# Two residual attention layers: diagonal blocks of a key-value product in column tiles, their copies on ScalarE, and pieces cut in two

## The reference

```python
xn = _ln(x, ln_w, ln_b)                                    # layer 0
q = softmax((xn @ Wq + bq).reshape(b, t, h, dh), axis=-1)
k = softmax((xn @ Wk + bk + (1 - mask) * -1e6).reshape(b, t, h, dh), axis=1)
v = ((xn @ Wv + bv) * mask).reshape(b, t, h, dh)
att = einsum('bnhd,bnhl->bhdl', k, v)
y = einsum('bnhd,bhdl->bnhl', q, att).reshape(b, t, d)
scale, shift = split((silu(emb) @ W_emb + b_emb)[:, None, :], 2, axis=2)
hh = _ln(y, ln2_w, ln2_b) * (1 + scale) + shift
x = x + silu(hh) @ W_out + b_out
# layer 1: the same frame, with att = softmax(q @ k.T + mask), y = att @ v, H = 16
```

## Time and profile before

| | |
|---|---|
| median of 3 runs | 870.1 us (869.51 to 870.53) |
| profiled execution, span | 869.6 us |
| TensorE busy | 825.9 us, 95% |
| VectorE busy | 786.1 us, 90% |
| ScalarE busy | 709.8 us, 82% |
| GpSimd busy | 732.7 us, 84% |
| granted TensorE clock, mean of the span | 0.987 |

### The profile page before, as it was taken

How to read it: one execution, slowest core, us unless ns; L and a number is a source line. 1 busy time by engine, 2 the same in 40 slices (tenths; PEclk the granted TensorE clock), 3 DMA queues, 4 the chain that set the end, 5 groups by cost and what they waited for, 6 DMA issues and landing times.

```text
span 869.6 us, 25205 instructions
## 1 busy us (share of the span) xinstructions
PE 825.9 (95%) x8653; PEld 590.2 (68%) x8653; DVE 786.1 (90%) x1610; ACT 709.8 (82%) x1250; POOL 732.7 (84%) x1214
## 2 busy tenths in 40 slices
PE   9998788999999999999999999999999999999885
PEld 4487666677777777777677777777777776656443
DVE  6898899999999999999999999999998999998962
ACT  6457847897889798888888888888888788998794
POOL 6769999799999989989999999988998887887314
PEclk8899989999999999999999999999999999999998
DMA  8221464435352525343534434334453333444311
GB/s 224 77 38 40 118 109 103 105 76 116 98 134 56 143 76 105 90 121 100 125 97 82 132 86 111 91 103 114 85 130 106 78 84 85 112 123 103 103 31 37
DMA packets 149306, 85.84 MB, mean 99 GB/s; under 512 B 87478, under 2 KB 141852, under 8 KB 149180
## 3 DMA queue, kind: packets, MB, share of 16 engines
q1 hardware_dynamic: 149180, 84.23, 39.5%
HBM read 39.52 MB, written 25.79 MB: 75 GB/s over the span
## 4 chain that ended last, share of the span: by engine, by line
PE 47%; POOL 18%; DVE 15%; issue 10%; ACT 4%; DMA 3%; SPq 2%; POOLq 0%; DVEq 0%; ACTq 0%
PE banks L690 12%; PE banks L837 7%; DVE NM L1274 6%; PE banks L698 5%; PE banks L824 4%; PE banks L813 4%; PE banks L705 3%; POOL Z L1933 2%; PE banks L720 2%; POOL ZHL L1940 2%; PE banks L847 2%; DVE st L1175 2%; POOL AB L2004 2%; PE banks L756 2%; POOL ZHL L1937 2%
## 5 line engine op out<-in xcount | busy, mean ns | idle before, releaser
L1274 DVE TENSOR_REDUCE NM<-banks 128x4 f32<-128x1024 f32 x256 | 302.5, 1212 | 9.5 <-PE banks L813 8.4
L1696 ACT ACTIVATE wraw<-banks,uu 128x1024 f32<-128x1024 f32 x154 | 170.2, 1136 | 22.3 <-PE banks L824 21.4
L1696 ACT ACTIVATE PX<-banks,uu 128x1024 f32<-128x1024 f32 x102 | 113.6, 1138 | 14.5 <-PE banks L824 12.8
L690 PE MATMUL banks<-wo,SH 128*128 128x256 f16 x768 | 96.1, 277 | 7.6 <-POOL SH L1978 7.2
L1920 POOL TENSOR_TENSOR rs<-ve,nhalf 128x2 f32<-128x2 f32 x128 | 90.2, 705 | 10.6
L813 PE MATMUL banks<-SK,SQ 51*128 51x256 f16 x1024 | 88.8, 273 | 7.0 <-DVE NM L1274 3.1
L824 PE MATMUL banks<-SQ,SK 53*128 53x256 f16 x1024 | 88.4, 272 | 6.9 <-DVE NM L1274 2.0
L690 PE MATMUL banks<-wv,ZT 128*128 128x256 f16 x768 | 94.5, 273 | 0.3 <-DVE AT L1224 0.2
L1978 POOL TENSOR_TENSOR SH<-ST,SH 128x512 f16<-128x512 f32 x64 | 74.3, 1168 | 22.9 <-ACT SH L1664 22.9
L690 PEld LDWEIGHTS banks<-wo,SH 128*128 128x128 f16 x768 | 73.2, 99 | 24.4 <-POOL SH L1978 10.5
L1678 ACT ACTIVATE R<-banks,fcs,sqs 128x256 f32<-128x256 f32 x128 | 73.8, 577 | 19.4 <-PE banks L698 19.2
(11 more groups left out here) (187 smaller groups left out, 1925.2 us busy)
## 6 DMA issues: line engine op xcount, KB each, us to landing
scr<-AB SPq DMA_DIRECT2D x64, 256.0 KB, 2.5
X<-in_x_dram SPq DMA_DIRECT2D x32, 256.0 KB, 2.9
SQ<-scr SPq DMA_DIRECT2D x64, 128.0 KB, 2.7
SK<-scr SPq DMA_DIRECT2D x64, 128.0 KB, 2.8
out_dram<-wemb SPq DMA_DIRECT2D x32, 256.0 KB, 2.5
SQ<-scr SPq DMA_DIRECT2D x64, 64.0 KB, 2.8
SK<-scr SPq DMA_DIRECT2D x64, 64.0 KB, 2.8
wemb<-in_L_cond_emb_w_dram SPq DMA_DIRECT2D x1, 1024.0 KB, 5.3
```

Of the source, the lines that this page charges most:

```text
L690: m = PE.matmul(dst[:, t, :], zt[:, j, k, t * P:(t + 1) * P], w[:, i, k, :], start=(k, n) == (0, 0), stop=(k, n) == (1, 2))
L1274: V.tensor_reduce(NMe[:, c, :, 2 * g:2 * g + 2], banks[:, n:n + 2, :].rearrange("p a (h m) -> p a h m", m=T), AX.X, ALU.max, negate=True). ...
L1696: A.activation(px(v % 5), banks[:, n:n + 2, :].rearrange("p a n -> p (a n)"), ACT.Exp, scale=uu[:, 0:1]).then_inc(S["exp"])
```

## The change

- `att`: only the diagonal blocks. For each half f and each token tile c, four products of 32x32 (j = 0 to 3), each writing 32 partitions and 32 columns of the bank, 16 products in place of 4.
- `at_` moves from VectorE to ScalarE: four copies of 32 partitions put the blocks on the diagonal of AT, whose other entries are set to zero once. The mask `blk` is gone. The keys' reciprocal sums are now applied in `qt`, in two halves with a scale per partition; `qt` waits for `rk` too.
- Pieces in two: statistics `s` and their aggregation `a` (VectorE); `r` loses the negated mean and the variance to ScalarE's new `n`; `z` becomes `c`, `h`, `z` (GpSimd), with one Z buffer for each layer; `km` leaves its scaling to GpSimd's `kn`, `np_` its first half to GpSimd's `nh`; `rq` is cut into `qd` and `rq`, `Y1_` into `rd` and `Y1_`.
- Setup: `mb3` and `mh3` share memory with PX2; constants `epa` are new.
- All five lists, the setup's order and the tables BANK and FREED are written anew. Their lines are left out below.

```diff
--- before.py
+++ after.py
...
         ident = sb("ident", [P, P])
-        blk = sb("blk", [P, P])
...
+        ve = sb("ve", [P, 2, 4, 2])
+        epa = sb("epa", [P, 2])
         nm = sb("nm", [P, 2, 4, 2])
         rs = sb("rs", [P, 2, 4, 2])
-        Z = sb("Z", [P, 2, D])
+        Z = sb("Z", [P, 2, 2, D])
...
             def x_in(b):
-                e.wait_ge(S["z0"], up(b - 2))
+                e.wait_ge(S["c0"], up(b - 2))
                 e.wait_ge(S["xb0"], up(b - 2))
                 e.dma_start(X[:, b % 3, :, :], x[b].rearrange("(t p) d -> p t d", p=P)).then_inc(d_x[b % 3], 16)
...
-                        m = PE.matmul(banks[:, n, f * P:(f + 1) * P], KTs[:, o, c, f * P:(f + 1) * P],
-                                      V0s[:, o, c, f * P:(f + 1) * P], start=(c == 0), stop=(c == 1))
+                        for j in range(4):
+                            h = slice(f * P + 32 * j, f * P + 32 * j + 32)
+                            m = PE.matmul(banks[32 * j:32 * j + 32, n, 32 * f:32 * f + 32], KTs[:, o, c, h], V0s[:, o, c, h],
+                                          start=(c == 0), stop=(c == 1))
                 m.then_inc(S["att"])
...
+            pv(4, 4); att(11); pv(4, 5); rows(6, 3); cols(4, 7); y0(10); y0T(9); y1T(3); rows(6, 4); rows(6, 5)
...
             def stats(b, l, src):
-                e.wait_ge(S[f"s{l}"], b)
+                e.wait_ge(S[f"a{l}"], b)
                 for t in range(2):
                     i = V.bn_stats(st[:, l, t, :], src[:, t, :])
-                follow(i)
+                i.then_inc(S[f"s{l}"])
+
+            def moments(b, l):
+
+                e.wait_ge(S[f"s{l}"], b + 1)
+                e.wait_ge(S[f"n{l}"], up(b - 1))
                 for t in range(2):
                     i = V.bn_aggr(mv[:, b % 2, l, t, :], st[:, l, t, :])
-                i.then_inc(S[f"s{l}"])
+                i.then_inc(S[f"a{l}"])
...
             def km(b):
                 e.wait_ge(S["k0"], b + 1)
-                e.wait_ge(S["ke"], b)
-                follow(V.tensor_reduce(kmx[:, :], bank(home("gk0", b)), AX.X, ALU.max, negate=True))
-                V.tensor_scalar(kmx[:, :], kmx[:, :], un[:, 1:2], None, ALU.mult).then_inc(S["km"])
+                e.wait_ge(S["kn"], b)
+                V.tensor_reduce(kmr[:, :], bank(home("gk0", b)), AX.X, ALU.max, negate=True).then_inc(S["km"])
...
             def rk(b):
                 e.wait_ge(S["ke"], b + 1)
+                e.wait_ge(S["qt"], up(b - 1))
                 V.reciprocal(rks[:, b % 2], ks[:, :]).then_inc(S["rk"])
...
+            def qd(b):
+                e.wait_ge(S["qe"], b + 1)
+                e.wait_ge(S["rq"], b)
+                V.tensor_reduce(qsum[:, :], heads(QE), AX.X, ALU.add).then_inc(S["qd"])
+
             def rq(b):
-                e.wait_ge(S["qe"], b + 1)
-                follow(V.tensor_reduce(qsum[:, :], heads(QE), AX.X, ALU.add))
+                e.wait_ge(S["qd"], b + 1)
+                e.wait_ge(S["Y0"], up(b - 1))
                 V.reciprocal(rqs[:, b % 2], qsum[:, :]).then_inc(S["rq"])
...
-            def at_(b):
-                e.wait_ge(S["att"], b + 1)
-                e.wait_ge(S["rk"], b + 1)
-                e.wait_ge(S["y0"], b)
-                for f in range(2):
-                    i = V.scalar_tensor_tensor(out=AT[:, f, :], in0=banks[:, home("gat", b), f * P:(f + 1) * P],
-                                               scalar=rks[:, b % 2, f:f + 1], in1=blk[:, :], op0=ALU.mult, op1=ALU.mult)
-                i.then_inc(S["at"])
-
...
             def np_(b):
-                e.wait_ge(S["max"], 8 * b + 8)
-                if b == 0:
-                    ready(e, "nmz")
-                else:
-                    e.wait_ge(d_nt[(b - 1) % 2], 16 * ((b - 1) // 2 + 1))
-                follow(V.tensor_scalar(NMp[:, :, 0, :], NM[:, :, :], 2.0 ** -15, None, ALU.mult))
+                e.wait_ge(S["nh"], b + 1)
                 V.scalar_tensor_tensor(out=NMp[:, :, 1, :], in0=NM[:, :, :], scalar=2.0 ** -15, in1=NMp[:, :, 0, :],
                                        op0=ALU.mult, op1=ALU.subtract).then_inc(S["np"])
 
+            def rd_(b, h):
+                v = banks[:, home(f"gty{h}", b), :].rearrange("p (c h f) -> p c h f", c=2, f=32)
+                e.wait_ge(S["ty"], 2 * b + h + 1)
+                if b >= 1:
+                    e.wait_ge(S["Y1"], 2 * b + h - 1)
+                V.reciprocal(rd[:, h], v[:, :, :, 16]).then_inc(S["rd"])
+
             def Y1_(b, h):
-                n = home(f"gty{h}", b)
-                e.wait_ge(S["ty"], 2 * b + h + 1)
+                e.wait_ge(S["rd"], 2 * b + h + 1)
                 e.wait_ge(S["yn1"], b)
-                v = banks[:, n, :].rearrange("p (c h f) -> p c h f", c=2, f=32)
-                follow(V.reciprocal(rd[:, h], v[:, :, :, 16]))
+                v = banks[:, home(f"gty{h}", b), :].rearrange("p (c h f) -> p c h f", c=2, f=32)
                 V.tensor_tensor(Y[:, 1].rearrange("p c (u h f) -> p u c h f", u=2, f=16)[:, h], v[:, :, :, 0:16],
                                 rd[:, h].unsqueeze(3).to_broadcast([P, 2, 8, 16]), ALU.mult).then_inc(S["Y1"])
...
+            def mean_of(b, l):
+                k, a = l % 2, (ZS ** -2, 1.0)[l % 2]
+                e.wait_ge(S[f"a{l}"], b + 1)
+                e.wait_ge(S[("c0", "yn0", "c1", "yn1")[l]], up(b - 1))
+                first(e, b, "cst")
+                A.activation(nm[:, b % 2, l, :], mv[:, b % 2, l, :, 0], ACT.Copy, scale=-1.0)
+                A.activation(ve[:, b % 2, l, :], mv[:, b % 2, l, :, 1], ACT.Identity, bias=epa[:, k:k + 1],
+                             scale=a).then_inc(S[f"n{l}"])
...
             def ke(b):
-                e.wait_ge(S["km"], b + 1)
+                e.wait_ge(S["kn"], b + 1)
...
             def qt(b):
                 e.wait_ge(S["qtT"], b + 1)
                 e.wait_ge(S["y0"], up(b - 1))
-                A.activation(QTs[:, b % 2], bank(home("gqt", b)), ACT.Identity).then_inc(S["qt"])
+                e.wait_ge(S["rk"], b + 1)
+                for f in range(2):
+                    i = A.activation(QTs[:, b % 2, f], bank(home("gqt", b))[:, f, :], ACT.Copy, scale=rks[:, b % 2, f:f + 1])
+                i.then_inc(S["qt"])
+
+            def at_(b):
+                first(e, b, "cst")
+                e.wait_ge(S["att"], b + 1)
+                e.wait_ge(S["y0"], b)
+                for j in range(4):
+                    h = slice(32 * j, 32 * j + 32)
+                    i = A.activation(AT[h, :, h], banks[h, home("gat", b), 0:64].rearrange("p (f n) -> p f n", f=2), ACT.Identity)
+                i.then_inc(S["at"])
...
 
             def norm(b, l):
 
-                a = (1.0, ZS ** -2)[l % 2 == 0]
-                e.wait_ge(S[f"r{l}"], b)
-                G.tensor_scalar(nm[:, b % 2, l, :], mv[:, b % 2, l, :, 0], -1.0, 0.0, ALU.mult, ALU.add)
-                follow(G.tensor_scalar(ve[:, l, :], mv[:, b % 2, l, :, 1], a, EPS * a, ALU.mult, ALU.add))
-                G.tensor_tensor(rs[:, b % 2, l, :], ve[:, l, :], nhalf[:, :], ALU.pow).then_inc(S[f"r{l}"])
+                e.wait_ge(S[f"n{l}"], b + 1)
+                e.wait_ge(S[("c0", "yn0", "c1", "yn1")[l]], up(b - 1))
+                G.tensor_tensor(rs[:, b % 2, l, :], ve[:, b % 2, l, :], nhalf[:, :], ALU.pow).then_inc(S[f"r{l}"])
...
-            def parts(b, l, src):
-
-                for i in range(2):
-                    e.wait_ge(S[f"z{i}"], turns[i])
-                turns[l] += 1
-                for t in range(2):
-                    i = G.tensor_scalar(Z[:, t, :], src[:, t, :], nm[:, b % 2, 2 * l, t:t + 1], rs[:, b % 2, 2 * l, t:t + 1], ALU.add, ALU.mult)
-                follow(i)
-                h, z = ZHL[:, l, b % 2], Z[:, :, :].rearrange("p t (k n) -> p t k n", k=2)
+            def centred(b, l, src):
+                e.wait_ge(S[f"r{2 * l}"], b + 1)
+                e.wait_ge(S[f"z{l}"], b)
+                apply(b, 2 * l, Z[:, l], src, f"c{l}")
+
+            def high(b, l):
+                e.wait_ge(S[f"c{l}"], b + 1)
+                if b >= 2:
+                    e.wait_ge(d_z[l][b % 2], 16 * (b // 2))
+                z = Z[:, l].rearrange("p t (k n) -> p t k n", k=2)
                 for k in range(2):
-                    i = G.tensor_scalar(h[:, 0, k], z[:, :, k, :], 1.0, 0.0, ALU.mult, ALU.add)
-                follow(i)
+                    i = G.tensor_scalar(ZHL[:, l, b % 2, 0, k], z[:, :, k, :], 1.0, 0.0, ALU.mult, ALU.add)
+                i.then_inc(S[f"h{l}"])
+
+            def remainder(b, l):
+                e.wait_ge(S[f"h{l}"], b + 1)
+                z = Z[:, l].rearrange("p t (k n) -> p t k n", k=2)
                 for k in range(2):
-                    i = G.tensor_tensor(h[:, 1, k], z[:, :, k, :], h[:, 0, k], ALU.subtract)
+                    i = G.tensor_tensor(ZHL[:, l, b % 2, 1, k], z[:, :, k, :], ZHL[:, l, b % 2, 0, k], ALU.subtract)
                 i.then_inc(S[f"z{l}"])
...
+            def kn(b):
```

(67 more changed lines are left out.)

988 lines of the change are left out of this document (504 added, 484 removed), and 220 rows, old and new, of the table FREED.

## The result

The changed kernel takes 842.98 us (median of 4 runs, 841.86 to 844.17) where the kernel before takes 870.32 (869.51 to 870.72) beside it. The ratio is 0.9679, 95% interval 0.9658 to 0.9701.

What follows compares the result with a forecast made beforehand. TensorE was taken as the bound in the middle, VectorE (95%) close behind. Span 869.6 - 8.3 (product) - 2 (VectorE) + 1 (ScalarE) = 860.3, plus 0.5 from profiled span to median: 860.8, called 861 us; range 851 to 880.

Steps and rivals of the forecast that it cites:

- Part 1: Key-value product `att` on TensorE: from 0.89 to 0.5 us a batch, 12.5 us gained, less 4.2 for changes of tiling.
- The pace rival: Small matmuls of `att` don't run at the burst's pace: no change, 868 to 876 us; chance 0.20.
- Part 2: VectorE loses 43.8 us of work; mostly worth nothing, 2 us off for TensorE's small waits, ends 0 and 6.
- part 4: GpSimd (net -39 us of work) and the queues: worth nothing; fill and end of the kernel also taken as 0.
- Net of part 1: -8.3 us: On TensorE, 12.5 us gained by the shorter `att` less 4.2 us for 42 more changes of tiling.
- the fast rival: More than the sum: cheaper `att`, 4 to 6 us from VectorE's waits, or a shorter fill; 848 to 853 us, chance 0.15.
- the low price of `att`: Key-value product on TensorE at 0.22 us a batch, the lower end: a gain of 21.4 us before 4.2 for tiling changes.
- Part 3: ScalarE gains small pieces, 2.06 us a batch, reaching 23.0 and 95% full; 1 us charged for added waiting.
- ScalarE becoming the bound: Rival: above 23.5 us of work a batch ScalarE sets the pace; slower, 879 us, chance 0.20.
- Fill and tail: Start and end of the kernel: fill taken as 0, ends -5 and +5 us; last batch's chain 0 within 0.3.

Runs made afterwards that it cites:

- two edits undone: Changed kernel with the full key-value product again and two more VectorE reductions of 672 ns a batch: 870.81 us, ratio 0.9965.
- three at 133.0: Changed kernel with the full key-value product, two more VectorE reductions a batch, and negated means and scaled variances back on GpSimd: 887.20 us, ratio 1.0186.
- the relief in the old order: Kernel before, old order, product tiled from batch 4, VectorE and GpSimd relieved by 48 and 47 us through work left out: 853.11 us, ratio 0.9787.

## Why the prediction was right and wrong, point by point

**The busy times: right.** ScalarE 771.2 us (775 forecast), VectorE 737.8 (742), GpSimd 685.3 (694). The four small kinds on ScalarE came to 61.4 us, 1.92 a batch against 2.06, though made of other prices than I had (the variance 307 ns and not 260, the mean 220 and not 160): the errors nearly cancelled in the overlap.

**Part 1, the price of the product: mis-sized at both ends, and by little.** I took 0.5 us a batch after and 0.89 before; from the first start to the next piece the medians are 0.39 and 0.99, and the 0.89 of the earlier trace rows is the shortest of the 32. The starts alone span 0.26 to 0.28 us. The loads' burst of 0.007 us in the earlier trace rows was the right row, but I charged it for loads and matmuls in turn. The matmuls alone go at 7 ns inside a round, and the loads run beside them. Over all batches the gain from start to start is 16.6 us and not 12.5 (two batches in the fill, with 3.2 and 1.6 us to the next piece, keep it below the medians' 19). The pace rival is out. Nor does this trace bear out, for parallel column tiles, the floor that the Trainium skill gives in *TensorE: Matmul & The Clock Gate*, "Wait — 56ns, not 53.3ns?": in four column tiles the starts stand at 9 ns and not 25. The changes of tiling rose by 44 (482 to 526) with those of the setup's narrow products, by 42 (480 to 522) without them, as I had; their sum of 4.2 us was not measured by itself.

**Part 2 and part 4, the value of the other engines' time: the step that failed.** "VectorE wasn't the bound, so most of this is worth nothing", 2 us, and "nothing" for GpSimd. In the old order, relieving the two without touching TensorE gives 12 us. In the new order 28 us put back on VectorE cost 14, and 40 put on GpSimd cost 10 (each load also makes a chain longer). The reading behind the step was a busy share of 98.7% for TensorE in the middle. That share is made from modelled ends of overlapping matmuls and covers short waits: the tiled product alone lowered it to 97.2%, with no change in time, and `cols` and `rows` took 10 us more from start to start for the same work. The waits in the earlier trace rows (16.4 against 3.5 us) told only of the longer ones. With four engines at 98.7, 95.0, 91.4 and 85.9%, in order and each waiting for the others, none is "the bound"; a loss anywhere is passed on in part. The waiting by which it is passed on is read from the starts and from these sums, not followed wait by wait.

**"Net of part 1: -8.3 us": right only beside the others.** The same edit is worth 0 in the old order alone, about 5 with the others relieved there, and 18 in the new order. As this term carried 8.3 of the forecast's 9.3 us, the right sign was in part luck. Terms priced one by one and added have no such answer. That is also why no rival held the result: the fast rival had the right direction (the low price of `att`, VectorE's waits, a shorter fill) with 4 to 6 us for VectorE and no fill in its sum.

**Part 3, ScalarE: the rival is out.** I gave 0.20 to ScalarE becoming the bound above 23.5 us of work a batch. It has 482.8 / 21.25 = 22.7 us in a period of 23.5, a share of 96.6%, just at the 96.5% from which I reckoned that rival's time; 8.4 us of busy time taken away gave nothing back. The charge of 1 us for 61 us of work was too low if the load tells the price: 10 us more of it, with a longer chain, cost 6. Whether that holds down to the first microsecond wasn't tried.

**Fill and tail: 0 taken, -13 found.** The first `cols` starts 13.2 us earlier, with 33.1 us of TensorE work between 80 and 120 us and not 29.9. With two edits undone it still starts at 128.8, with three at 133.0, and with the relief in the old order at 137.4: most of it is the new order's doing. The next four batches give 4.9 back. My ends of 5 us were too narrow for an order that had been rewritten from the first line on, and the prediction gave the rewriting no term.

**What stays open.** Every load and every relief here changes an engine's work and the length of a chain of results at once, and no run parts the two. What is shown is that time on VectorE and GpSimd isn't free; whether its price is that of a full queue or of a longer chain is not. Nor can the parts of the gain be divided cleanly. From the old order with the reliefs and the tiled product (853.1) the new order brings 9 us; from the new order with three edits undone (887.2) the edits bring 44. Neither path has exactly the same work at its corner, and in the new order a load costs between a quarter and nearly all of what it adds while a relief (ScalarE's) brings nothing. That fits an order laid out for exactly these durations, but it was only argued: no order was planned anew for other durations. Nor was any run made with the new order and the pieces uncut, or with one Z buffer, so what these give by themselves is not known.
